# A hybrid SSD, attention and Mamba network on one core: gelus ahead of exponentials, two copies moved to VectorE, and the scan's next inputs formed at the end of a pair

## The reference, cut to what matters

```python
x = x + ssd(layernorm(x))        # a state-space block
x = x + ffn(layernorm(x))        # "layers": depth 2
x = x + mamba(layernorm(x))      # a selective scan: 256 channels, 16 states, sequential in time
x = x + ffn(layernorm(x))        # the same two layers once more
```

```python
q, k, v = split(shift_token(x) @ wqkv)
q, k = rotary(l2norm(q) * qs, l2norm(k) * ks)
x = x + softmax(masked(q @ k.T)) @ v @ wo
h = layernorm(shift_token(x)) * lg + lb
a, g = split(h @ w1 + b1)        # 341 + 341 hidden features
x = x + (a * gelu(g)) @ w2 + b2
```

## Time and profile before

| | us |
|---|---|
| median of 3 runs | 2646.31 (2639.4 to 2657.2) |
| the profiled execution, its own time | 2651.16 |
| its span, first to last instruction | 2649.4 |
| PE, DVE, ACT, POOL busy | 2192.8, 1996.1, 1856.4, 1543.0 |
| mean granted TensorE clock | 0.928 of full speed |

### The profile page before, as it was taken

The page is one execution under the profiler, slowest core; times in us unless marked ns, Lnnn a source line. Parts: engine busy times, 40 slices in busy tenths (PEclk is TensorE's granted clock), DMA queues, the critical chain, the costliest instruction groups (busy, mean ns, idle before and its releaser), DMA issues. The chain is left out here.

```text
span 2649.4 us, 46209 instructions
## 1 busy us (share of the span) xinstructions
PE 2192.8 (83%) x13308; PEld 1124.7 (42%) x13308; DVE 1996.1 (75%) x5421; ACT 1856.4 (70%) x4745; POOL 1543.0 (58%) x1364
## 2 busy tenths in 40 slices
PE   5888789999999999667777767776799899999997
PEld 2555445455555555222222222222355455555553
DVE  4666477777777776388998989898677777787774
ACT  3555277778777777488687777776677777777774
POOL 1233276556665665177787677676565556665652
PEclk8999799999999999788888888889999999999999
DMA  3000000000000000000000000000000000000000
GB/s 129 1 0 1 4 13 13 10 14 12 13 13 14 12 9 14 0 0 1 1 1 1 0 1 0 0 1 0 13 13 13 9 14 12 13 17 17 21 13 17
DMA packets 12209, 30.04 MB, mean 11 GB/s; under 512 B 2240, under 2 KB 2240, under 8 KB 11584
## 3 DMA queue, kind: packets, MB, share of 16 engines
q1 hardware_dynamic: 11968, 27.41, 3.8%
HBM read 8.52 MB, written 2.10 MB: 4 GB/s over the span
## 5 line engine op out<-in xcount | busy, mean ns | idle before, releaser
L517 POOL TENSOR_TENSOR arena<-arena 128x512 f32<-128x512 f32 x256 | 325.0, 1270 | 444.8 <-DVE arena L1530 444.8
L575 POOL TENSOR_TENSOR arena<-arena 128x512 f32<-128x512 f32 x256 | 327.7, 1295 | 127.2 <-ACT arena L1257 118.5
L523 POOL TENSOR_TENSOR arena<-arena,SR 128x512 f32<-128x512 f32 x256 | 285.3, 1114 | 109.5 <-ACT SR L1139 108.6
L1610 DVE TENSOR_TENSOR_SCAN arena<-arena,psum 128x512 f32<-128x512 f32 x256 | 311.0, 1215 | 3.2
L929 PE MATMUL psum<-BS,tabs 96*128 96x512 bf16 x384 | 146.1, 442 | 197.1 <-DVE arena L1610 195.3
L997 PE MATMUL psum<-arena,first 128*128 128x512 f32 x512 | 288.8, 653 | 10.9 <-POOL arena L566 10.6
L1536 DVE TENSOR_REDUCE SM<-arena 128x8 f32<-128x512 f32 x256 | 175.6, 686 | 155.9 <-ACT arena L1129 145.5
L530 POOL TENSOR_TENSOR P<-P,RS 128x512 f32<-128x512 f32 x256 | 270.3, 1056 | 35.5 <-DVE RS L1457 35.1
L1129 ACT ACTIVATE arena<-psum 128x512 f32<-128x512 f32 x256 | 151.4, 591 | 186.6 <-PE psum L853 186.5
L853 PE MATMUL psum<-rest,HA 128*128 128x512 f32 x512 | 267.3, 604 | 0.4 <-DVE HA L1445 0.4
L807 PE MATMUL psum<-HN,rest 128*128 128x512 f32 (+1 forms) x384 | 197.0, 640 | 56.0 <-ACT arena L1122 51.0
(11 more groups left out here) (223 smaller groups left out, 5290.8 us busy)
## 6 DMA issues: line engine op xcount, KB each, us to landing
arena<-arena SPq DMA_DIRECT2D x128, 128.0 KB, 2.3
rest<-in_rest SPq DMA_DIRECT2D x1, 4183.0 KB, 20.9
X<-in_x SPq DMA_DIRECT2D x1, 2048.0 KB, 9.0
out<-X SPq DMA_DIRECT2D x8, 256.0 KB, 2.3
tabs<-in_tabs SPq DMA_DIRECT2D x1, 1216.0 KB, 11.5
first<-in_first SPq DMA_DIRECT2D x1, 875.5 KB, 4.5
```

The costliest lines, as they stand in the source:

```text
L517: nc.gpsimd.tensor_tensor(CQ[:, n % 2, :], CQ[:, n % 2, :], SQN[:, n % 2, :], ALU.add).then_inc(f_rope, 1)
L523: nc.gpsimd.tensor_tensor(heads, heads, SR[:, n % 2, :].unsqueeze(2).to_broadcast([128, HEADS, DH]), ALU.mult).then_inc(f_qk, 1)
L575: nc.gpsimd.tensor_tensor(WU[:, k % DEEP, :], RG[:, k % DEEP, :], U[t.j % 2][:, k % 2, :], ALU.mult).then_inc(m_wu, 1)
L1610: v.tensor_tensor_scan(HS[:, k % DEEP, :], AB[:, k % DEEP, :], B_BANK[k % 2], 0.0, ALU.mult, ALU.add).then_inc(m_hs, 1)
```

## The change

In the layers, `gelus` (g = 5) now stands ahead of `exponentials` on ACT; `norms` stands ahead of `features` at each item; the `features` of h = 21 moves to DVE, where it and `flipped(5)` now stand ahead of `reciprocals(6)`; and `gated(0)` moves from h = 22 to h = 25. In the scan, the first two WU products of the next pair and its first three spreads are issued at the end of a turn, ahead of the last sums; the pool's and PE's last steps are reordered around them; and three parts of `dve_beginning` stand one step later.

```diff
--- before.py
+++ after.py
@@ -565,15 +565,19 @@
                 t.wait_ge(m_acc, STEPS, k + 1 - DEEP)
                 nc.gpsimd.tensor_tensor(PC[:, k % DEEP, :], HS[:, k % DEEP, :], CS[:, s % 2, :], ALU.mult).then_inc(m_pco, 1)
 
+            def weighted_input(t, k, pair=0):
+                t.wait_ge(m_rg, STEPS, k + 1, pair=pair)
+                t.wait_ge(m_vb, STEPS, k + 1 - DEEP, pair=pair)
+                if k == 0:
+                    t.wait_ge(m_u, 1, 1, pair=pair)
+                nc.gpsimd.tensor_tensor(WU[:, k % DEEP, :], RG[:, k % DEEP, :], U[(t.j + pair) % 2][:, k % 2, :],
+                                        ALU.mult).then_inc(m_wu, 1)
+
             def pool_turn(t):
                 for k in range(STEPS):
                     if t.states:
-                        t.wait_ge(m_rg, STEPS, k + 1)
-                        t.wait_ge(m_vb, STEPS, k + 1 - DEEP)
-                        if k == 0:
-                            t.wait_ge(m_u, 1, 1)
-                        nc.gpsimd.tensor_tensor(WU[:, k % DEEP, :], RG[:, k % DEEP, :], U[t.j % 2][:, k % 2, :],
-                                                ALU.mult).then_inc(m_wu, 1)
+                        if k >= 2:
+                            weighted_input(t, k)
                         if k % 2 == 0 and k >= 4:
                             odd_times_c(t, k // 2 - 2)
                     if not t.after:
@@ -591,9 +595,11 @@
                         t.wait_ge(m_xi, 2, 2, pair=1)
                         t.wait_ge(m_wu, STEPS, STEPS, pair=-1)
                         nc.gpsimd.tensor_tensor(U[(t.j + 1) % 2][:, :, :], LV[:, :, :], XI[:, :, :], ALU.mult).then_inc(m_u, 1)
-                if t.states:
-                    odd_times_c(t, NS - 2)
-                    odd_times_c(t, NS - 1)
+                for late in range(2):
+                    if t.after:
+                        weighted_input(t, late, pair=1)
+                    if t.states:
+                        odd_times_c(t, NS - 2 + late)
 
             pairs(pool, pool_turn)
             pool.wait_ge(m_x, PAIRS)
@@ -925,19 +931,19 @@
             layers_pe(0)
             pe.wait_ge(f_x, PAIRS)
 
-            def spread(t, s, column, dst, done):
-                mm(dst, T16("sel", 128 * column, 128 * column + 128, p=96), BS[t.j % 2][:, :],
+            def spread(t, column, dst, done, pair):
+                mm(dst, T16("sel", 128 * column, 128 * column + 128, p=96), BS[(t.j + pair) % 2][:, :],
                    start=True, stop=True).then_inc(done, 1)
 
-            def spread_b(t, k):
-                t.wait_ge(m_hs, STEPS, k - 1)
+            def spread_b(t, k, pair=0):
+                t.wait_ge(m_hs, STEPS, k - 1, pair=pair)
                 if k == 0:
-                    t.wait_ge(m_bs, 3, 3)
-                spread(t, k, k // 2, B_BANK[k % 2], m_bb)
-
-            def spread_c(t, s):
-                t.wait_ge(m_pce, NS, s - 1)
-                spread(t, s, NS + s, C_BANK[s % 2], m_bc)
+                    t.wait_ge(m_bs, 3, 3, pair=pair)
+                spread(t, k // 2, B_BANK[k % 2], m_bb, pair)
+
+            def spread_c(t, s, pair=0):
+                t.wait_ge(m_pce, NS, s - 1, pair=pair)
+                spread(t, NS + s, C_BANK[s % 2], m_bc, pair)
 
             def half_sum(k, weight, source, done):
                 last = mm(STAT, weight(k), source[:, k, :], start=k == 0, stop=k == 1)
@@ -1001,9 +1007,6 @@
 
             def pe_turn(t):
                 if t.states:
-                    spread_b(t, 0)
-                    spread_c(t, 0)
-                    spread_b(t, 1)
                     spread_c(t, 1)
                 for k in range(STEPS):
                     if t.states:
@@ -1015,11 +1018,15 @@
                         pe_ending(t, k)
                     if t.after:
                         pe_beginning(t, k)
-                    if t.states and k >= 2:
+                    if t.states and 2 <= k < STEPS - 1:
                         accumulate(t, k - 2)
+                if t.after:
+                    spread_b(t, 0, pair=1)
+                    spread_c(t, 0, pair=1)
+                    spread_b(t, 1, pair=1)
                 if t.states:
-                    accumulate(t, STEPS - 2)
-                    accumulate(t, STEPS - 1)
+                    for k in range(STEPS - 3, STEPS):
+                        accumulate(t, k)
 
             pairs(pe, pe_turn)
             pe.wait_ge(m_x, PAIRS)
@@ -1157,10 +1164,10 @@
                     inverse_root(inner, inner_at, STAT, LSQ[:, :])
                 if item(k, h, 1):
                     squares(k, *item(k, h, 1))
-                if item(k, h, 7):
-                    features(k, *item(k, h, 7))
                 if item(k, h, 3):
                     norms(k, *item(k, h, 3))
+                if item(k, h, 7) and h // 4 != 5:
+                    features(k, *item(k, h, 7))
                 if k.pre and h in (14, 30):
                     values(k, (14, 30).index(h) + 2)
 
@@ -1168,11 +1175,11 @@
                 for g in range(8):
                     if k.pre and g in (1, 2):
                         values(k, g - 1)
+                    if k.post and g == 5:
+                        gelus(k)
                     if k.heads(g + 1):
                         exponentials(k, *k.heads(g + 1), 0)
                         exponentials(k, *k.heads(g + 1), 1)
-                    if k.post and g == 5:
-                        gelus(k)
                     if k.heads(g) and g != 5:
                         flipped(k, *k.heads(g))
                     for h in range(4 * g, 4 * g + 4):
@@ -1475,6 +1482,12 @@
                 k.wait_ge(f_ptp, 8, g + 1, slot=m)
                 v.tensor_copy(PT[:, g % 2, :], P_BANK).then_inc(f_pta, 1)
 
+            def features(k, m, n):
+                tt, part = divmod(n, 2)
+                k.wait_ge(f_xp, 8, n + 1, slot=m)
+                v.tensor_copy(QKT[k.side(m)][:, 4 * part:4 * part + 4, 128 * tt:128 * tt + 128],
+                              T_BANK.rearrange("p (c t) -> p c t", t=128)).then_inc(f_qkt, 1)
+
             def after_attention(k):
                 r = R[:, k.tokens(-1)]
                 k.wait_ge(f_at, 1, 1, slot=-1)
@@ -1559,7 +1572,7 @@
                         centre(inner, inner_at, HF[:, :], STAT, CEN[:, :])
                     elif h == 15:
                         normalise(inner, inner_at, CEN[:, :], LSQ[:, :], HN[:, :])
-                    elif h == 22:
+                    elif h == 25:
                         gated(k, 0)
                     elif h == 26:
                         gated(k, 1)
@@ -1582,10 +1595,12 @@
                     dve_dense(k, 4 * g + 1)
                     if k.heads(g + 2):
                         maxima(k, *k.heads(g + 2), 1)
+                    if k.heads(g) and g == 5:
+                        flipped(k, *k.heads(g))
+                    if g == 5 and item(k, 21, 7):
+                        features(k, *item(k, 21, 7))
                     if k.heads(g + 1):
                         reciprocals(k, *k.heads(g + 1))
-                    if k.heads(g) and g == 5:
-                        flipped(k, *k.heads(g))
                     dve_dense(k, 4 * g + 2)
                     dve_dense(k, 4 * g + 3)
 
@@ -1636,16 +1651,16 @@
                     STT(xs, STAT, out_bias_b[:, :], xs, ALU.add, ALU.add).then_inc(m_x, 1)
 
             def dve_beginning(t, k):
-                if k == 2:
+                if k == 3:
                     t.wait_ge(ln_mean, 1, LN_M + 1, pair=1)
                     TT(CEN[:, :], X[:, t.tokens(1)], SIDE, ALU.subtract).then_inc(ln_cen, 1)
-                elif k == 8:
+                elif k == 9:
                     t.wait_ge(ln_rs, 1, LN_M + 1, pair=1)
                     t.wait_ge(ln_cen, 1, LN_M + 1, pair=1)
                     t.wait_ge(m_bp, 1, 1)
                     t.wait_ge(m_zp, 2, 2)
                     TT(HN[:, :], CEN[:, :], LRS[:, :], ALU.mult).then_inc(ln_out, 1)
-                elif k == 11:
+                elif k == 12:
                     t.wait_ge(m_exp, 1, 1, pair=1)
                     t.wait_ge(m_ld, 1, 1)
                     TS(WV[:, :, :], AV[:, :, :], 1.0, None, ALU.add).then_inc(m_w, 1)
```

## The result

| | before | after |
|---|---|---|
| median, us (runs of one chip) | 2650.53 (2639.4 to 2657.2, 4 runs) | 2683.87 (2680.61 to 2685.39, 4 runs) |
| ratio, 95% interval | | 1.0121 [1.0096, 1.0146] |
| span of the profiled execution, us | 2649.4 | 2681.6 |
| PE, DVE, ACT, POOL busy, us | 2192.8, 1996.1, 1856.4, 1543.0 | 2203.8, 2023.4, 1842.7, 1539.4 |
| mean granted TensorE clock | 0.928 | 0.927 |

The change costs 32 us by the ratio (25 to 39) and 32.2 by the spans. The forecast was +19.2, the predicted time 2666. DVE's last residual update of each slot divides the program (before against after, from the timelines of DVE): up to the first one +2.2; first pass over the layers 667.6 against 690.6, +23.0; from there to the second pass, the scan in it, 875.7 against 858.9, -16.8; second pass 670.3 against 694.2, +23.9. The layers lose almost three times what the scan wins.

The account below looks back on a forecast made before the run. PE was taken to bound the layer slots and DVE the scan turns. Terms +26.0 + 1 - 7.8 = +19.2 us, against a median of 2646, gave 2666 us; the forecast's own range was 2653 to 2686, the whole range 2600 to 2695.

Parts of the forecast that it names:

- the layers' 27: Layers: the late gate product's 26.0 us over 28 steady slots, plus 1 for slots at the ends of a pass.
- a few falls of the clock: Layers: TensorE falling to its lower level in a few slots, allowed for only in the range 2653 to 2686.
- a rival of 0.12: Layers: the clock falls in most slots, 1.5 us each with no cover, 28 times, +42, 2708 us; chance 0.12.
- Gate product, +0.93 a slot: Layer slot: the third other_half tile waits for gated(0) at h = 25, so project(6) starts 0.93 us later; 28 slots, 26.0.
- The gap moves and does not go: Layer slot: PE's 1.69 us wait for the gelu shrinks to 0.15, but PE idles about 2.1 before flip(6).
- The copies cost nothing on DVE: Layer slot: two copies of 0.67 us each fit DVE's idle time before the exponentials end and remove PE's 0.46.
- The ends of a pass, +1: Slots at the ends of a layer pass: fewer instructions between, +1 us.
- Scan, the change of turn, -19.7: Scan, change of turn: inputs formed during DVE's last scan remove its waits, 14.2 + 5.5 us won.
- Scan, the centring, +11.9: Scan turn: centring a step later, behind DVE's wait at line 1627, delays ACT, then POOL; 1.7 us in seven turns.
- The scan's sum, -7.8: Whole scan: -19.7 at the change of turn plus 11.9 for the centring, -7.8 us.

Follow-up runs that it names:

- the two halves: The kernel before with only the change's layer edits: 1.018, 48 us slower; and with only its scan edits: 0.9962, 10 us faster.
- after_warm: The changed kernel plus two matmuls, result unread, filling PE's gap before the flip of g = 6: 2669.89 us, 1.0079 to the kernel before.
- after_warm_g22: The changed kernel plus the two filling matmuls and gated(0) back at h = 22: 2643.98 us, 0.9981 to the kernel before.

## Why the prediction was wrong, step by step

It had the sign, the moved gap and the late gate product. Its sum was 13 us too small: 19.2 for a measured 32. By the medians of the two halves (+48 and -10) it was the layers' 27 that fell short, by about 21: the clock is about 11 of them, the ends of the passes 7 and the size of the slot's term 3.

- **The step that failed: "a few falls of the clock".** The sum adds nothing for the clock and makes its fall in most slots a rival of 0.12. It fell in 21 of 28. Spans of steady slots tell its price: over the 26 steady intervals of both passes the kernel after is 38.7 longer than the kernel before, after_warm, where the clock falls behind no flip, 23.5. The falls cost 15.2 us, 0.6 a slot in the mean and 0.9 where the clock falls for the whole stretch (47.4 against 46.5). The kernel before paid for falls of its own, about 0.7 each (46.2 against 45.5) in six of these intervals, and they are gone in the kernel after; what the change adds is therefore about 11 us. The rival's price of 1.5 "with no cover" was near the 1.7 measured without the late product. The argument against the rival was that a gap of 1.69 had mostly left the clock alone. But the gap moved to another place and grew: 2.15 in front of the flip and 0.34 behind it, with the short transposes between, where before the third gate tile's full matmuls followed. Which of these differences matters no run separates; that filling the gap ends the falls is shown. Before, the clock fell in 7 of 28 slots, not in the four that the prediction counted (the group took 2.93 to 3.59 there), and such a row was the warning. The section "HAM oscillation" of the Trainium skill's page "TensorE: Matmul & The Clock Gate", which the prediction cites, tells of waits for transfers that are longer than this gap and drop the clock every time; the gap of 2.15 did so in 21 of 28 slots.
- **Gate product, +0.93 a slot: about right, and hidden.** Where the clock falls in neither kernel, a slot of after_warm is 1.04 longer than one of the kernel before (46.52 against 45.48): 0.80 go when `gated(0)` goes back (45.72 in after_warm_g22), and 0.24 stay with the later transposes. The wait is 0.58 in the row for 0.7 forecast. PE does have two short waits later in the slot, for POOL (0.34 and 0.48 before), but as forecast they absorb nothing. In the kernel after it mostly does not show: PE runs late, and the wait stands in 7 of the 28 slots, those in which the clock did not fall. Its price and the clock's do not add.
- **The gap moves and does not go: right.** The wait for the gelu fell to 0.22 (forecast 0.15), the one in front of the flip is 2.15 (2.1), with POOL as its releaser, as said. The copies cost nothing on DVE: it waits 2.22 behind them. `squares(5)` starts 7.75 after `squares(4)`; 7.7 was forecast.
- **The ends of a pass, +1: too small.** The last full slot of each pass went from 35.0 to 38.5; with the last ones (0.6 and 0.5), about +8. In the slot before last there are no projections of a next pair to cover the exponentials. PE there, in the kernel after:

```profile
1090.71 0.66 PE L769 MATMUL psum<-first,P 128*128 128x128 f32 x4 [3.15 <-POOL P L530]
```

  Before, this flip had no such gap. I had called these slots neutral because fewer instructions lie between, and the opposite follows: fewer instructions cover the wait.
- **Scan, the change of turn, -19.7: about right.** The runs give -17.5 for the inputs formed ahead. At the second jump of the hardware loop DVE waits 1.59 for issue and for nothing else (at the first, 1.36 for a spread):

```profile
1598.63 0.70 DVE L1619 TENSOR_TENSOR psum<-arena,psum 128x512 f32<-128x512 f32 x1 [1.59 <-issue]
```

- **Scan, the centring, +11.9: oversized, with one link wrong.** The runs give about +7 for all three parts together, and with the copies in place no difference for the centring. The forecast had DVE wait for PE's sum at line 1627. It does not. PE in the kernel before at the start of a turn, then after:

```profile
1497.02 1.91 PE L943 MATMUL psum<-arena,first 128*128 128x512 f32 x2
1498.73 1.92 PE L965 MATMUL psum<-X,first 128*128 x2
```

```profile
1513.11 1.02 PE L949 MATMUL psum<-arena,first 128*128 128x512 f32 x2
1513.97 1.02 PE L971 MATMUL psum<-X,first 128*128 x2
```

  Before, a gap of 2.51 at the change of turn had left these at the lower level; with it gone they take half the time, and the sum is there before DVE asks. So it is in five of the six turns in the middle of the scan; in the other the clock falls here in the kernel after too. A moved gap that costs the clock in the layers gives it back here. What the prediction's mechanism does show is ACT's longer wait for the centred tokens (5.7 for 4.2), and POOL's at step 20 (1.75 here and 1.07 at step 22; 0.69 before, near 3 forecast):

```profile
1555.43 0.70 DVE L1619 TENSOR_TENSOR psum<-arena,psum 128x512 f32<-128x512 f32 x1 [1.75 <-POOL arena L573]
...
1561.42 0.69 DVE L1619 TENSOR_TENSOR psum<-arena,psum 128x512 f32<-128x512 f32 x1 [1.07 <-POOL arena L573]
```

- **The scan's sum, -7.8,** lies inside the runs' -10 (-5 to -15). The profiled executions showed -16.8 in the stretch between the passes: one of them need not be typical for the scan, since line 1669 takes 1.6 or 5.3 from turn to turn.

## What to carry to other kernels

When a reordering moves a stall of TensorE, price the clock at its new place as its own term of the sum: a granted clock that already dips in some slots is a warning that a longer gap may make it dip in most. Count the dips in all slots, and in more than one execution: with the layers unchanged they came in 7 to 12 of 28 slots. When two costs lie behind one another, undo both before judging either. And of a bundle of edits try each alone: here the copies and the scan's inputs were worth 1%, and the gelus' move and the late gate product together took 2%.

## What was unexpected in the hardware

- A repeated gap of 2.15 with 0.34 behind it dropped the clock in 21 of 28 slots; one of 1.69 followed by full matmuls in 7 of 28 (7 to 12 over five executions). Two matmuls in the gap (1.98 us together), whose result nobody reads, kept it up behind all 28 flips and won 11 us.
- A VectorE instruction of 128x1024 with its operands in SBUF took 0.75 in the scan's first turn, where GpSimd forms no products, 1.6 when it waited for one product, and 5.3 when it fell into a row of them: in most turns it waits through four, and GpSimd then stands still while it runs.
